# Linear attention and FFN on one core: x loaded nine tiles ahead, and three turns of 32x32 blocks put in another order

## What is computed

```
q = exp(x Wq^T + bq);  k = exp(x Wk^T + bk);  v = x Wv^T + bv        per head
num[s] = sum over t <= s of (q[s].k[t]) v[t];   den[s] = q[s] . (sum over t <= s of k[t])
x1 = layernorm(x + (num/den) Wo^T + bo)
y  = layernorm(x1 + tanh(x1 (W A1 A2) + bias))
```

## Time and profile before

| | us |
|---|---|
| median of 3 runs | 2465.79 (2458.34 to 2468.32) |
| the profiled execution | 2467.03, its span 2465.3 |
| PE busy, matmuls | 2321.6 (94%) |
| DVE busy | 1797.8 (73%) |
| POOL busy | 1314.3 (53%) |
| ACT busy | 1052.8 (43%) |
| DMA | 241.90 MB, mean 98 GB/s |

### The profile page before, as it was taken

One profiled execution on the slowest core, in us unless ns is written; L12 is line 12 of the kernel. 1 busy time (PEld: TensorE's weight loads), 2 busy tenths in 40 slices (PEclk: granted clock), 3 DMA queues, 4 the chain that ended last, 5 costly groups with the idle time before them and its releaser, 6 DMA issues.

```text
span 2465.3 us, 58596 instructions
## 1 busy us (share of the span) xinstructions
PE 2321.6 (94%) x21040; PEld 1907.9 (77%) x21040; DVE 1797.8 (73%) x2710; ACT 1052.8 (43%) x2039; POOL 1314.3 (53%) x1669
## 2 busy tenths in 40 slices
PE   6999999999999999999999999999999999999985
PEld 5778878877877887777777877777777877777764
DVE  4677777777777777777777777777777777777664
ACT  3434444444444444444444444444444444444431
POOL 1455555555655555555555555554555555555553
PEclk9999999999999999999999999999999999999998
DMA  6233333333333333333333333333333333333211
GB/s 162 71 98 103 106 99 102 103 98 96 105 100 100 103 100 97 104 98 99 102 97 100 102 99 100 102 99 99 99 101 100 100 102 99 98 103 96 64 65 52
DMA packets 293918, 241.90 MB, mean 98 GB/s; under 512 B 32848, under 2 KB 225360, under 8 KB 293712
## 3 DMA queue, kind: packets, MB, share of 16 engines
q1 hardware_dynamic: 293712, 238.69, 30.9%
HBM read 139.99 MB, written 98.57 MB: 97 GB/s over the span
## 4 chain that ended last, share of the span: by engine, by line
PE 93%; issue 4%; DVE 1%; ACT 1%; DMA 0%; SPq 0%; POOL 0%; POOLq 0%; ACTq 0%; DVEq 0%
PE G L310 25%; PE G L312 24%; PE G L311 24%; PE SC L377 6%; PE G L389 5%; PE G L364 4%; PE G L410 2%; PE G L401 1%; PE G L411 1%; PE SC L310 0%; PE SC L312 0%; PE SC L311 0%; DMA QT<-wqT 0%; DVE o L656 0%; SPq L272 0%
## 5 line engine op out<-in xcount | busy, mean ns | idle before, releaser
L775 POOL TENSOR_TENSOR qk1L<-WK,qk1H 128x512 fp32r<-128x512 f32 x128 | 165.4, 1292 | 814.7 <-ACT qk1H L555 814.7
L679 DVE RECIPROCAL o<-G 128x512 f32<-128x512 f32 x128 | 424.9, 3320 | 2.8 <-PE G L411 1.4
L673 DVE STREAM_TRANSPOSE SC<-WK 128x512 f32<-128x512 f32 x128 | 93.0, 727 | 448.5 <-DMA WK<-x_rows 448.5
L753 POOL TENSOR_SCALAR_AFFINE_SELECT A<-A 128x512 f32<-128x512 f32 x512 | 314.4, 639 | 10.7 <-issue 6.6
L517 ACT ACTIVATE A<-SC 128x512 f32<-128x512 f32 x512 | 275.3, 591 | 61.1 <-PE G L389 59.7
L792 POOL TENSOR_TENSOR xTL<-xin,xTH 128x512 fp32r<-128x512 f32 x128 | 164.8, 1288 | 245.6 <-ACT xTH L568 245.5
L310 PE MATMUL G<-WfH,x1H 128*128 128x512 f32 x512 | 211.1, 412 | 83.4 <-issue 71.7
L555 ACT ACTIVATE qk1H<-WK 128x512 fp32r<-128x512 f32 x128 | 81.0, 633 | 469.6 <-DVE WK L707 469.6
L724 DVE TENSOR_SCALAR WK<-xres,mv,rstd 128x512 f32<-128x512 f32 x128 | 200.5, 1566 | 86.4 <-POOL rstd L782 86.4
L533 ACT ACTIVATE x1H<-SC 128x512 fp32r<-128x512 f32 x128 | 76.6, 599 | 374.0 <-DVE SC L673 374.0
L310 PE MATMUL G<-xTH,WqH 128*128 128x512 f32 x512 | 203.0, 396 | 28.7 <-POOL xTL L792 21.1
(11 more groups left out here) (107 smaller groups left out, 5597.2 us busy)
## 6 DMA issues: line engine op xcount, KB each, us to landing
xin<-x SPq DMA_DIRECT2D x512, 64.0 KB, 1.9
xres<-x SPq DMA_DIRECT2D x128, 256.0 KB, 3.3
x_rows<-WK SPq DMA_DIRECT2D x128, 256.0 KB, 2.1
WK<-x_rows SPq DMA_DIRECT2D x512, 64.0 KB, 2.0
out<-WK SPq DMA_DIRECT2D x128, 256.0 KB, 2.1
k_rows<-WK SPq DMA_DIRECT2D x120, 256.0 KB, 2.3
WK<-k_rows SPq DMA_DIRECT2D x480, 64.0 KB, 2.0
QT<-wqT SPq DMA_DIRECT2D x4, 256.0 KB, 4.2
```

The source lines that it names most:

```text
L679: nc.vector.reciprocal(oflat, den_ps[:, :]).then_inc(recip_ready, 1)
L753: last = nc.gpsimd.affine_select(out=A[:, j, :, :], in_=A[:, j, :, :], compare_op=ALU.is_ge, fill=0.0, base=0, pattern=[[0, NK], [1, P]], ...
L775: nc.gpsimd.tensor_tensor(qk1L[:, :], WK[:, 7, :], qk1H[:, :].bitcast(F32), ALU.subtract).then_inc(qk1l_ready, 1)
```

## The change

- SP loads x nine tiles ahead instead of eight (SP has 9 slots ahead, the other engines still 8), and in its slot the K store and K load come first, then the x load, the output store, the x1 store, the x1 load, and last the xres load, which now has a wait of its own for `x1_ready`.
- DVE turns x (tile k+8) before the reciprocal instead of near the slot's end, and turns x1 behind the reciprocal instead of ahead of it; the second layernorm's last step goes ahead of `x1L`.
- The loop has one chunk fewer, and the last two chunks are written out.

No instruction's size or count changes.

```diff
--- before.py
+++ after.py
@@ -42,7 +42,7 @@
     Q_SHIFT = 8.0
 
     XIN = 2
-    assert B == 2 * QUAD and NI >= 3
+    assert B == 2 * QUAD and NI >= 4
 
     x_t = x.rearrange("b (i p) d -> b i p d", p=P)
     x_b = x.rearrange("b (i t p) (a f) -> b i a p t f", t=P // HD, p=HD, a=HG)
@@ -222,11 +222,11 @@
                 slot(Chunk(t // B), t % B)
                 if t in setup:
                     setup[t]()
-            with nc.Fori(1, NI - 1, engines=(engine.engine,), hint_back_edge=True) as it:
+            with nc.Fori(1, NI - 2, engines=(engine.engine,), hint_back_edge=True) as it:
                 c = Chunk(it, engine)
                 for k in range(B):
                     slot(c, k)
-            for t in range(NT - B, NT + behind):
+            for t in range(NT - 2 * B, NT + behind):
                 slot(Chunk(t // B), t % B)
 
         block = ctx.enter_context(nc.Block())
@@ -264,8 +264,15 @@
                 sp.dma_start(wo_raw, wview(woT)).then_inc(wo_loaded, 16)
 
             def slot(c, k):
-                if c.exists(k + 8):
-                    n = k + 8
+                if c.updates_state(k):
+                    wait_before(sp, (k_turned, c.count(k + 1)))
+                    sp.dma_start(k_rows, KS).then_inc(k_stored[k % B], 16)
+                    wait_before(sp, (k_stored[k % B], c.dma_count(k)), (state_done, c.count(k)))
+                    for j in range(HG):
+                        sp.dma_start(Ktok[j * HD:(j + 1) * HD, :].rearrange("p (a c) -> p a c", a=HG),
+                                     k_blocks[j]).then_inc(ktok_loaded[k % B], 16)
+                if c.exists(k + 9):
+                    n = k + 9
 
                     wait_before(sp, (xl_ready, c.count(n - 1)))
                     for j in range(HG):
@@ -275,29 +282,23 @@
                     n = k - 3
                     wait_before(sp, (out_ready, c.count(n + 1)))
                     sp.dma_start(out_t[n % B, c.it + n // B], y[:, n % 2, :]).then_inc(out_stored[n % B], 16)
-                if c.updates_state(k):
-                    wait_before(sp, (k_turned, c.count(k + 1)))
-                    sp.dma_start(k_rows, KS).then_inc(k_stored[k % B], 16)
-                    wait_before(sp, (k_stored[k % B], c.dma_count(k)), (state_done, c.count(k)))
-                    for j in range(HG):
-                        sp.dma_start(Ktok[j * HD:(j + 1) * HD, :].rearrange("p (a c) -> p a c", a=HG),
-                                     k_blocks[j]).then_inc(ktok_loaded[k % B], 16)
                 n = k - 1
                 if c.exists(n):
                     wait_before(sp, (x1_ready, c.count(k)))
                     sp.dma_start(x1_rows, x1[:, n % 2, :]).then_inc(x1_stored[n % B], 16)
-                if c.exists(k + 1):
-                    if c.static() and c.it * B + k == -1:
-                        sp.wait_ge(c_done, 1)
-                    m = k + 1
-                    sp.dma_start(xres[:, m % 2, :], x_t[m % B, c.it + m // B]).then_inc(xres_loaded[m % B], 16)
                 if c.exists(n):
                     wait_before(sp, (x1_stored[n % B], c.dma_count(n)), (x1_turned, c.count(n)))
                     for j in range(HG):
                         sp.dma_start(x1s[j * HD:(j + 1) * HD, :].rearrange("p (t f) -> p t f", t=HG),
                                      x1_blocks[j]).then_inc(x1s_loaded[n % B], 16)
-
-            run_slots(sp, slot, 8, 3, {-7: load_wq_and_biases, -5: load_wk, -4: load_ffn_weights_and_wv,
+                if c.exists(k + 1):
+                    if c.static() and c.it * B + k == -1:
+                        sp.wait_ge(c_done, 1)
+                    wait_before(sp, (x1_ready, c.count(k)))
+                    m = k + 1
+                    sp.dma_start(xres[:, m % 2, :], x_t[m % B, c.it + m // B]).then_inc(xres_loaded[m % B], 16)
+
+            run_slots(sp, slot, 9, 3, {-7: load_wq_and_biases, -5: load_wk, -4: load_ffn_weights_and_wv,
                                        -2: load_wo})
             for n in range(B):
                 sp.wait_ge(out_stored[n], 16 * NI)
@@ -665,27 +666,32 @@
                     nc.vector.transpose(KS[:, :].rearrange("p (t g f) -> p g t f", t=HG, f=HD),
                                         KT[:, (k // QUAD) % 2, :, cols].rearrange("p g (t q) -> p g t q", q=HD)
                                         ).then_inc(k_turned, 1)
-                if ffn:
-                    n = k - 2
-                    wait(dve, x1s_loaded[n % B], c.part_count(n))
-
-                    wait(dve, scores_out[0], c.count(k + 1))
-                    nc.vector.transpose(x1T_ps.rearrange("p (g t q) -> p g t q", g=NK, q=HD),
-                                        x1s[:, :].rearrange("p (t g f) -> p g t f", t=HG, f=HD)).then_inc(x1_turned, 1)
+                if c.exists(k + 8):
+                    m = k + 8
+                    wait(dve, xin_loaded[m % B], c.part_count(m))
+                    xblocks = xin[:, m % XIN, :]
+                    nc.vector.transpose(xblocks, xblocks).then_inc(x_turned, 1)
                 if att:
                     wait(dve, den_done, c.count(k + 1))
                     wait(dve, oh_ready, c.count(k))
                     wait(dve, ol_ready, c.count(k))
                     nc.vector.reciprocal(oflat, den_ps[:, :]).then_inc(recip_ready, 1)
                 if ffn:
+                    n = k - 2
+                    wait(dve, x1s_loaded[n % B], c.part_count(n))
+
+                    wait(dve, scores_out[0], c.count(k + 1))
+                    nc.vector.transpose(x1T_ps.rearrange("p (g t q) -> p g t q", g=NK, q=HD),
+                                        x1s[:, :].rearrange("p (t g f) -> p g t f", t=HG, f=HD)).then_inc(x1_turned, 1)
+                if fin:
+                    wait(dve, rstd2_ready, c.count(k - 2))
+                    nc.vector.tensor_scalar(yf, yf, mv2[:, 0:1], rstd[:, 1:2],
+                                            ALU.subtract, ALU.mult).then_inc(out_ready, 1)
+                if ffn:
                     wait(dve, x1h_ready, c.count(k - 1))
                     nc.vector.tensor_tensor(x1L[:, :, :].rearrange("p g q -> p (g q)"), x1T_ps,
                                             x1H[:, :, :].rearrange("p g q -> p (g q)").bitcast(F32),
                                             ALU.subtract).then_inc(x1l_ready, 1)
-                if fin:
-                    wait(dve, rstd2_ready, c.count(k - 2))
-                    nc.vector.tensor_scalar(yf, yf, mv2[:, 0:1], rstd[:, 1:2],
-                                            ALU.subtract, ALU.mult).then_inc(out_ready, 1)
                 n = k + 1
                 nb, nq = n % B, (n // QUAD) % 2
                 ncols = slice(n % QUAD * P, (n % QUAD + 1) * P)
@@ -723,11 +729,6 @@
                     wait(dve, y_ready, c.count(k - 2))
                     nc.vector.tensor_scalar(x1[:, (k - 1) % 2, :], r, mv1[:, 0:1], rstd[:, 0:1],
                                             ALU.subtract, ALU.mult).then_inc(x1_ready, 1)
-                if c.exists(k + 8):
-                    m = k + 8
-                    wait(dve, xin_loaded[m % B], c.part_count(m))
-                    xblocks = xin[:, m % XIN, :]
-                    nc.vector.transpose(xblocks, xblocks).then_inc(x_turned, 1)
                 if ffn:
                     wait(dve, y_ready, c.count(k - 1))
                     nc.vector.bn_stats(bnst[:, 1, :], y[:, k % 2, :]).then_inc(bn2_ready, 1)
```

More of the change, by code:

```diff
@@ L667, in slot @@
                                         ).then_inc(k_turned, 1)
+                if c.exists(k + 8):
[3 more added lines that the diff above has]
+                    nc.vector.transpose(xblocks, xblocks).then_inc(x_turned, 1)
+                if att:
+                    wait(dve, den_done, c.count(k + 1))
+                    wait(dve, oh_ready, c.count(k))
+                    wait(dve, ol_ready, c.count(k))
+                    nc.vector.reciprocal(oflat, den_ps[:, :]).then_inc(recip_ready, 1)
                 if ffn:
```

## The result

The changed kernel takes 2382.8 us (2382.0 to 2386.15, 4 runs), the kernel before in the same comparison 2466.07: a ratio of 0.967 (95% interval 0.965 to 0.9689), faster by 3.3%. The forecast was 2381, in a range of 2360 to 2412. The profiled execution took 2383.27 us, its span 2381.5, against 2467.03 and 2465.3: 83.8 us less.

A forecast was written before the change was run, and what follows sets the result against it. PE was taken to be held by a circle of waits over the reciprocal and x1's memory trip. Terms -93.3 (loop), -10 (outside), +6 (remaining waits), +12.5 (start) sum to -84.8 us: 2381, range 2360 to 2412.

The forecast's parts named there:

- What bounds the kernel: PE's loop slots: 17.61 us of work, but a circle over x1L, x1's memory trip and the reciprocal sets 18.5.
- The reciprocal ahead, and oL forward by 1.2: DVE and POOL in each slot: oL ends near +4.95 instead of +6.13, x1L near +10.3, before PE wants it at +11.16.
- The loop's stretch: Scores of tile 8 to tile 120: 93.3 us less from waits and one loop turn, 6 us left for remaining waits.
- The slot of four with ACT's late copy: One slot in four: the running sum waits for ACT's K copy; next slot's x1L ends about +10.7, ahead of +11.16.
- The second layernorm beside POOL: DVE's layernorm meeting POOL's L771 costs 1.0 us more; at worst 24 us in all, 6 taken.
- Rival (a): DVE's second layernorm and POOL meet on shared ports in every slot: 24 us instead of 6, 2399; chance 0.12.
- K's trip, x load, xres: all hidden: SP's new queue order: K's earlier trip gains nothing, the x load and the roughly 4 us later xres cost nothing.
- Outside the stretch: Early tiles and last chunk: FFN waits of 13.4 us shrink by 10, bounds 5 and 13.4.
- The start: Weight loads behind the extra x tile: Wq 4.8 us later, Wk at 26.3 instead of 11.79; costs 12.5, bounds 4.8 and 16.
- The range: Whole run, 2360 to 2412: low end no waits, full 13.4 outside, start at 4.8; high end half of (b).
- (b): oL stays at +6.13, held by something else on POOL: 49 us of waits in place of 6, 2424; chance 0.10.

## Why the prediction was right, point by point

- **What bounds the kernel.** Right: PE's work is 17.6 us a slot, and a circle over the reciprocal and x1's trip made 18.5 of it. Either half of the new order alone left the loop at about 18.3 us a tile (18.35 and 18.26).
- **The reciprocal ahead, and oL forward by 1.2.** Right to 0.2 us at every station from oL on, in a slot without a wait (xTL came 0.6 earlier than forecast). That PE's wait closes in most slots is shown, and so is that both parts are needed. Where the remaining wait would sit with the reciprocal's place alone I had wrong before that run (q, not the FFN).
- **The loop's stretch.** -93.3 + 6 = -87.3 forecast, -84.3 measured. The total hides two errors of a size, and that they cancel is luck. I left 0.9 us for each of 12 turns of PE's loop, 10.8 in all; that gap is gone. And I left 6 us for remaining waits; they are 20 (from start to start). About half of these go with DVE's own jump back, which I hadn't costed at all although every engine has the same loop; xres's place accounts for another 10 (1981.8 us of stretch with xres ahead again).
- **The slot of four with ACT's late copy.** The delay of DVE was right (1.7 us). That it "ends ahead of +11.16" in the next slot was right alone and wrong together with the jump back or with a late layernorm; taking 1.25 us of it away gave 13 us, more than the 6 I had for all that remains.
- **The second layernorm beside POOL.** The term that was mis-sized. The forecast had L771 (now L772) over by +8.3, though it had xres land at +7 to +8 and L771 takes 1.3 us. It began at +8.34 in the median, waiting for xres, so it often still ran when the layernorm began at about +9.0 (+9.5 in the fifth slot of a turn). The rows of before gave 1.0 us as the price where they meet; it was anything up to 1.1, by how far they overlap. In 39 of the stretch's 112 slots the layernorm lasted 0.81 to 1.62 us instead of 0.50, and in every one of these it ended 0.28 us behind L772. Rival (a) had a chance of 0.12; it happened in part and cost 11 of its 24 us. The Trainium skill ("SBUF — State Buffer", Who interferes with whom) states that whichever of the two issues first holds the shared ports for its whole instruction and the other is blocked meanwhile. The trace agrees that the later one ends only behind the earlier; that it then needs 0.28 us and not its full 0.50, that sentence doesn't explain.
- **K's trip, x load, xres: all hidden.** Right for the first two. Wrong for xres, by 11 us, through the layernorm above.
- **Outside the stretch.** 10 forecast, 11.5 measured.
- **The start.** 12.5 forecast, 12.0 measured. Wq and Wk went out within 0.1 us of the forecast; the product of the FFN's matrices came at 50.79 of the 48.6 to 51.0 that were given, near the end that had the half clock in it.
- **The range.** Its ends don't follow from what was named: the low end adds up to 2364, not 2360, and half of (b) is 2402, not 2412. The measured time is far from both.

## What to carry to other kernels

Draw the circle of waits that comes back to itself one tile later and add it up: as long as it is longer than the busiest engine's slot, removing one wait moves it to another place of the circle. When it has become shorter, look at each engine's jump back and at each instruction that is late once in several tiles, since two small delays that cost next to nothing alone meet there. And when a load is moved in a queue, look at the start of the program as well: here one more tile ahead put 12 us of weight loads onto the path, which one line gives back.

## What was not expected of the hardware

- DVE stood for about 1.0 us behind each jump back of its loop (13.2 us with the loop's entry, 0.3 with the slots written out). PE's 0.65 us of idle time at the same place is not there in the changed kernel. That it needs a wait of PE just ahead of it is not shown: with the reciprocal's place alone it was still 5.1 us in 13 turns, though the FFN had no wait in those slots.
- A 256 KB load issued ahead of four 64 KB loads of another tensor cost these 0.16 us of their way (3.89 against 3.73 us to the turning).
- From the x1 store to the issue of the load that waits for it were 2.1 us in five slots of eight and 3.4 to 3.7 in three, in the mean (kernel before; single ones 2.8 to 4.3). The trace shows what the long ones have in common: the core's DMA engines also move its instructions, 16 KB at a time. Of 110 stores, 40 took over 2.6 us to land, and in each of these such a transfer started within 1.8 us of the store's issue; the 61 stores without one took 2.02 to 2.14 us. Nine more had one, all but one of them late (1.58 us or more behind the issue), and took 2.07 to 2.56 us. Queue lines of a long store (1022.12 to 1025.63) and of a short one (1040.95 to 1043.02):

```profile
q1 hardware_dynamic: 285, 0.52, 43.4%
q8 instruction: 1, 0.02, 2.5%
...
q1 hardware_dynamic: 179, 0.33, 48.4%
```

  No run moved these transfers, so that they are the cause is not shown. By an estimate from these times, (3.6 - 2.1) x 3/8 = 0.5 to 0.6 us per tile, they would be over half of the 0.9 us by which the circle of the kernel before was longer than PE's work.
